# The triangular inverse of a gated delta rule: its levels on the changing half of the columns, eight units per instruction

## The chip, the cores and the metric

The kernel runs on one core of one Trainium2 chip. The time is the device time in microseconds, the median of three runs of the whole program. The profile is one execution of the same program, taken by the hardware profiler.

## The reference

The reference is one attention layer of the gated delta rule with a residual and a layer norm, followed by a feed-forward layer on ternary weights with another residual and layer norm. The input is 8 sequences of 512 tokens with 256 features. There are 16 key heads, each with 2 value heads, of width 128.

The core of it takes the sequence in chunks. For each chunk and head it forms a strictly lower triangular matrix M from the keys, their gates and a decay, and needs T, the inverse of (I - M):

```python
M = -jnp.tril(jnp.einsum('bhnik,bhnjk->bhnij', k_beta, k) * decay, k=-1)
T = solve_triangular(eye - M, jnp.broadcast_to(eye, M.shape), lower=True)
v_new = jnp.einsum('bhnij,bhnjd->bhnid', T, v_beta)
k_cumdecay = jnp.einsum('bhnij,bhnjd->bhnid', T, k_beta * jnp.exp(g)[..., None])
```

A scan over the chunks then carries a state of 128x128 per head: the inverse is applied to the values less what the state predicts, the state is updated with the result, and the output is the part from the state and the part from within the chunk. The kernel uses chunks of C = 128, so 4 chunks per sequence.

## The kernel before

The program has three blocks: the gates, the delta rule, the feed-forward layer. The delta rule is a loop over 128 items, one for each of 16 key heads and 8 sequences. An item has 4 chunks and 2 heads, so 8 units of 128x128.

Each pass of the loop works on three items at once, in three streams. "early" prepares the next item: splitting operands, four projections K, Q, V0, V1 (L516), the projection z (L526), tap and convolution, norms, transposes, Gram matrices (L553). "late" inverts the current item's matrices. "back" runs the recurrence of the item before: per chunk the state product `ks_mm` (L631), the residual (L893), the product with the inverse `y` (L647), its copy `y_copy` (L779), the state update (L660, L910), the query products (L637, L673) and the output; then the norm `o_norm` (L929), transposes `o_turn` (L686) and the output product (L693). `qs_mm` is L637, `intra` is L673.

The inverse is built by doubling. It starts with blocks of 2x2 and has six levels, l = 0 to 5; level l joins blocks of size s = 2 << l into blocks of 2s. U and T, its transpose, are held in f16 in `u16_` and `t16_`, the rounded matrix in `a16`. A level has three products, each on eight units: P from `a16` and T (L593); then, after a mask has picked the off-diagonal blocks of P into `pl[l]`, which is preset to the identity (L865), the new T from U and `pl[l]` (L603) and the new U from `pl[l]` and U (L607). The eight units are handled as two groups g0 and g1 of four, since four units of 128 columns in f32 fill one bank of PSUM, the memory that TensorE writes to. So a level has 6 batches of four matmuls, two predicated copies on VectorE, and four copies back: T of g0 on VectorE (L870), T of g1 (L768) and both U (L771) on ScalarE. After the last level a residual product (L617) and a correction (L624) sharpen the result.

Every engine executes its steps in one fixed order, written out by hand in `ORDER`, with `level(l)` for levels 0 to 3, where the recurrence of the item before lies between the steps. Levels 4 and 5 lie among the projections K, Q and V0 of the next item. Semaphores guard each hand-over: `p_mm`, `p_ready`, `t_mm`, `u_mm`, `t_ready`, `u_ready`.

## Time and profile before

| | us |
|---|---|
| median of 3 runs | 5981.18 |
| lowest, highest | 5980.92, 5990.64 |
| span of the profiled execution | 5983.6 |
| TensorE busy | 5351.0 (89%) |
| VectorE busy | 4743.2 (79%) |
| ScalarE busy | 4155.5 (69%) |
| GpSimd busy | 3081.8 (52%) |

The span is the time from the first to the last instruction of the profiled execution; no other time of that execution is given. An engine's busy time is the union of its instructions' records. A matmul's record holds its own latency, and records overlap when matmuls follow each other, so starts tell more than lengths: "x4" with 0.39 us is four matmuls whose last record ends 0.39 us after the first one's start. "PEld" is the load of the stationary operand. An engine's idle time is listed with what ended it.

### The profile page before, as it was taken

To read this page: it belongs to the slowest core of one execution; us is meant where nothing else is said; L and a number is where in the kernel's file an instruction comes from. 1 tells how busy PE (TensorE), PEld (TensorE's weight loads), DVE (VectorE), ACT (ScalarE), POOL (GpSimd) and SP (SyncE) were. 2 spreads that over 40 slices of the span, in tenths; PEclk is the share of its full clock that TensorE was granted. 3 is DMA by queue.
4 is the path that set the end of the run, shared out by engine and by line. 5 is a ranking of instruction groups with operands and counts; after the bars stand their busy time and mean duration, and the time that the engine had idled before them with its cause. 6 is when DMAs were issued, how large, how long until landed. Compare 5 with 4: busy or idle time off the path is not lost. (4 is left out here: it accounts for less than half of the span.)

```text
span 5983.6 us, 146544 instructions
## 1 busy us (share of the span) xinstructions
PE 5351.0 (89%) x45450; PEld 4415.7 (74%) x45578; DVE 4743.2 (79%) x8288; ACT 4155.5 (69%) x10963; POOL 3081.8 (52%) x3690
## 2 busy tenths in 40 slices
PE   2899999999999999999999999999999999999867
PEld 2677777777777777777777777777777777777756
DVE  4788888888888888888888888888888888888754
ACT  1677777777777777777777777777777777777634
POOL 0555555555555555555555555555555555555434
PEclk8999999999999999999999999999999999999988
DMA  3010101010101010100101010101010101010000
GB/s 105 31 36 27 36 27 36 27 36 27 36 27 36 27 36 27 36 27 30 32 27 36 27 36 27 36 27 36 27 36 27 36 27 36 27 36 27 18 29 21
DMA packets 130814, 194.64 MB, mean 33 GB/s; under 512 B 13344, under 2 KB 61600, under 8 KB 130464
## 3 DMA queue, kind: packets, MB, share of 16 engines
q1 hardware_dynamic: 129312, 190.78, 10.0%
q14 instruction: 325, 2.66, 0.1%
q10 hardware_dynamic: 1152, 0.79, 0.1%
q8 instruction: 25, 0.41, 0.0%
HBM read 185.75 MB, written 5.77 MB: 32 GB/s over the span
## 5 line engine op out<-in xcount | busy, mean ns | idle before, releaser
L865 DVE CAST_PREDICATED pl<-masks,pa 128x512 f16<-128x512 uint16 x1536 | 983.6, 683 | 84.3 <-PE pa L593 84.2
L771 ACT ACTIVATE u<-pa 128x512 f16<-128x512 f32 x1536 | 924.5, 602 | 16.2 <-PE pa L607 8.2
L824 DVE SCALAR_TENSOR_TENSOR conv<-pb,cws,conv 128x511 f32<-128x511 f32 (+2 forms) x1152 | 831.5, 740 | 65.6 <-ACT conv L714 65.6
L1001 POOL TENSOR_TENSOR xo<-xo,zs 128x512 f32<-128x512 f32 x256 | 327.5, 1279 | 745.1 <-DVE xo L923 745.1
L516 PE MATMUL pb<-xb,wb 128*128 128x512 f32 x2304 | 626.6, 407 | 1.7 <-POOL xb L995 1.7
L603 PE MATMUL pa<-pl,u 128*128 128x128 f16 x6144 | 602.7, 221 | 3.0 <-DVE pl L865 3.0
L607 PE MATMUL pa<-u,pl 128*128 128x128 f16 x6144 | 595.1, 219 | 0.0
L779 ACT ACTIVATE yb<-pb 128x256 f32<-128x256 f32 x512 | 196.7, 384 | 531.2 <-PE pb L647 372.5
L593 PE MATMUL pa<-t,a 128*128 128x128 f16 x6144 | 495.4, 220 | 73.7 <-DVE t L858 72.8
L870 DVE CAST t<-pa 128x512 f16<-128x512 f32 x768 | 527.1, 686 | 1.7 <-PE pa L603 1.3
L593 PEld LDWEIGHTS pa<-t,a 128*128 128x128 f16 x6144 | 388.3, 98 | 189.8 <-DVE attn L838 48.3
L603 PEld LDWEIGHTS pa<-pl,u 128*128 128x128 f16 x6144 | 395.0, 98 | 148.7 <-issue 76.2
L768 ACT ACTIVATE t<-pa 128x512 f16<-128x512 f32 x768 | 462.4, 602 | 57.0 <-PE pa L603 53.1
L693 PE MATMUL pb<-wout,xt 128*128 (+1 forms) x2048 | 493.1, 384 | 2.1 <-ACT xt L800 2.1
L714 ACT ACTIVATE conv<-pb,cws 128x512 f32<-128x512 f32 x384 | 265.2, 691 | 322.0 <-PE pb L516 317.5
L516 PEld LDWEIGHTS pb<-xb,wb 128*128 128x128 f32 x2304 | 405.8, 189 | 68.4 <-POOL xb L995 2.0
L607 PEld LDWEIGHTS pa<-u,pl 128*128 128x128 f16 x6144 | 408.8, 98 | 0.0
L693 PEld LDWEIGHTS pb<-wout,xt 128*128 128x128 f32 x2048 | 370.2, 191 | 42.8 <-ACT xt L800 2.8
L526 PE MATMUL pa<-wb,xb 128*128 128x256 f32 x3072 | 399.6, 286 | 0.0
L893 DVE SCALAR_TENSOR_TENSOR res<-pb,small,vt 128x128 f32<-128x128 f32 x768 | 234.1, 346 | 187.8 <-PE pb L631 183.8
L526 PEld LDWEIGHTS pa<-wb,xb 128*128 128x128 f32 x3072 | 376.1, 191 | 0.0
L647 PE MATMUL pb<-res,u 128*128 128x128 f32 x2048 | 336.9, 287 | 31.2 <-DVE res L889 30.5
(171 smaller groups left out, 13882.1 us busy)
## 6 DMA issues: line engine op xcount, KB each, us to landing
tokn<-in_Wqkvz SPq DMA_DIRECT2D x256, 256.0 KB, 2.7
conv<-in_xT SPq DMA_DIRECT2D x256, 256.0 KB, 3.3
conv<-in_Wqkvz SPq DMA_DIRECT2D x128, 256.0 KB, 2.8
gxb<-in_xT SPq DMA_DIRECT2D x8, 512.0 KB, 3.6
wout<-in_W_out SPq DMA_DIRECT2D x1, 4096.0 KB, 17.7
yacc<-in_x_tok SPq DMA_DIRECT2D x2, 2048.0 KB, 20.6
out<-fob SPq DMA_DIRECT2D x8, 512.0 KB, 2.9
lrow<-rows_scratch SPq DMA_DIRECT2D x128, 6.0 KB
```

Source lines behind the costliest of these rows:

```text
L516: last = nc.tensor.matmul(proj_bank[c][:, :], wb[:, pw, k * WCOL + c * D:k * WCOL + (c + 1) * D], xb[:, px, k * S:(k + 1) * S], start=(i = ...
L526: last = nc.tensor.matmul(proj_bank[4 + g][:, n * R * D:(n + 1) * R * D], xb[:, px, at:at + C], wb[:, pw, k * WCOL + 4 * D:(k + 1) * WCOL] ...
L593: last = nc.tensor.matmul(pa[2 * g + 1][:, u * C:(u + 1) * C], a16[:, 4 * g + u, :], t16_[:, 4 * g + u, :], start=True, stop=True)
L603: last = nc.tensor.matmul(pa[2 * g + 1][:, u * C:(u + 1) * C], u16_[:, 4 * g + u, :], pl[l][:, 4 * g + u, :], start=True, stop=True)
L607: last = nc.tensor.matmul(pa[2 * g][:, u * C:(u + 1) * C], pl[l][:, 4 * g + u, :], u16_[:, 4 * g + u, :], start=True, stop=True)
L647: last = nc.tensor.matmul(pb[0][:, h * D:(h + 1) * D], u32[p][:, unit(n, h), :], res[:, h, :], start=True, stop=True)
L693: last = nc.tensor.matmul(pb[3][:, i * H:(i + 1) * H], xt[:, unit(2 * g + i, h), :], wout[:, ds((b // B) * R + h, 1), :].rearrange("p a n ...
L768: nc.scalar.activation(group(t16_, g), four(pa[2 * g + 1]), ACT.Copy)\
L771: nc.scalar.activation(group(u16_, g), four(pa[2 * g]), ACT.Copy).then_inc(u_ready[g].sem, 1)
L824: nc.vector.scalar_tensor_tensor(out=conv[c][:, back:S], in0=proj_bank[c][:, 0:S - back], scalar=cws[p][:, c * TAPS + 3 - back:c * TAPS + ...
L865: nc.vector.copy_predicated(group(pl[l], g), masks[:, l:l + 1, :].broadcast_to([128, 4, C]), four(pa[2 * g + 1])).then_inc(p_ready.sem, 1)
L870: nc.vector.tensor_copy(group(t16_, 0), four(pa[1])).then_inc(t_ready[0].sem, 1)
```

## The change

A level changes only half of the columns: of T those of the first block of each pair, of U those of the second. After the change the products P, T and U of a level stream just these 64 columns of each unit, and write them packed, so that all eight units (8 x 64 = 512 values in f32) fit in one bank: P in `pa[3]`, T in `pa[1]`, U in `pa[0]`. Each product has one copy for all eight units, that spreads the packed columns back to their places: `halves(t, l, odd)` takes of every unit the pieces of s = 2 << l elements that lie 2s apart. The predicated copy stays on VectorE, both copies back are ScalarE's, and the second group's waits are gone or merged. T and U become separate steps, with the state update of the recurrence between them. In the diff, lines of the order table beyond these and lines that only pass names on are left out.

```diff
+        def halves(t, l, odd):
+
+            return t[:, :, :].rearrange("p u (b w s) -> p u b w s", w=2, s=2 << l)[:, :, :, odd, :]
+
+        def half_unit(t, u, l, odd):
+
+            return t[:, u, :].rearrange("p (b w s) -> p b w s", w=2, s=2 << l)[:, :, odd, :]
+
+        def packed(bank, l):
+
+            return bank[:, :].rearrange("p (u b s) -> p u b s", u=NU, s=2 << l)
+
+        def packed_unit(bank, u):
+
+            return bank[:, u * (C // 2):(u + 1) * (C // 2)]
...
-        u_first, t_first_mm, p_mm, p_ready, t_mm, u_mm = signal("u_first", 2), signal("t_first_mm", 2), signal("p_mm", 12), signal("p_ready", 12), signal("t_mm", 12), signal("u_mm", 12)
-        u_ready = [signal(f"u_ready{g}", LEVELS) for g in range(2)]
-        t_ready = [signal(f"t_ready{g}", LEVELS + 1) for g in range(2)]
+        u_first, t_first_mm, p_mm, p_ready, t_mm, u_mm = signal("u_first", 2), signal("t_first_mm", 2), signal("p_mm", LEVELS), signal("p_ready", LEVELS), signal("t_mm", LEVELS), signal("u_mm", LEVELS)
+        u_ready, t_ready, t_first_ready = signal("u_ready", LEVELS), signal("t_ready", LEVELS), signal("t_first_ready", 2)
+        p_bank, t_bank, u_bank = pa[3], pa[1], pa[0]
...
-                    + (back(("q_part", l)) if l and chain else []) + late(("p", l), ("ut_mm", 2 * l)) + (back(("update_mm", l)) if l < NC - 1 else [])
-                    + late(("ut_mm", 2 * l + 1)) + (back(("intra_mm", l)) if chain else []) + sum(between, []) + late(("ut", l))
+                    + (back(("q_part", l)) if l and chain else []) + late(("p", l), ("t_mm", l)) + (back(("update_mm", l)) if l < NC - 1 else [])
+                    + late(("u_mm", l)) + (back(("intra_mm", l)) if chain else []) + sum(between, []) + late(("t_copy", l), ("u_copy", l))
...
             def p_product(a, p, l):
-                for g in range(2):
-                    pe.wait_ge(t_ready[g].sem, t_ready[g].at(a, l + 1))
-                    if l == 0 and g == 0:
-                        pe.wait_ge(attn_ready.sem, attn_ready.at(a, 2))
-                    if l == 0 and g == 1:
-                        pe.wait_ge(vt_ready.sem, vt_ready.at(a, 1))
-                    for u in range(4):
-                        last = nc.tensor.matmul(pa[2 * g + 1][:, u * C:(u + 1) * C], a16[:, 4 * g + u, :],
-                                                t16_[:, 4 * g + u, :], start=True, stop=True)
-                    last.then_inc(p_mm.sem, 1)
-
-            def ut_product(a, p, i):
-                l, g = i // 2, i % 2
-                pe.wait_ge(p_ready.sem, p_ready.at(a, i + 1))
+                if l == 0:
+                    pe.wait_ge(t_first_ready.sem, t_first_ready.at(a, 2))
+                    pe.wait_ge(attn_ready.sem, attn_ready.at(a, 2))
+                    pe.wait_ge(vt_ready.sem, vt_ready.at(a, 1))
+                else:
+                    pe.wait_ge(t_ready.sem, t_ready.at(a, l))
+                for u in range(NU):
+                    last = nc.tensor.matmul(packed_unit(p_bank, u), a16[:, u, :], half_unit(t16_, u, l, 0), start=True, stop=True)
+                last.then_inc(p_mm.sem, 1)
+
+            def t_product(a, p, l):
+                pe.wait_ge(p_ready.sem, p_ready.at(a, l + 1))
                 if l:
-                    pe.wait_ge(u_ready[g].sem, u_ready[g].at(a, l))
-                for u in range(4):
-                    last = nc.tensor.matmul(pa[2 * g + 1][:, u * C:(u + 1) * C], u16_[:, 4 * g + u, :],
-                                            pl[l][:, 4 * g + u, :], start=True, stop=True)
+                    pe.wait_ge(u_ready.sem, u_ready.at(a, l))
+                for u in range(NU):
+                    last = nc.tensor.matmul(packed_unit(t_bank, u), u16_[:, u, :], half_unit(pl[l], u, l, 0), start=True, stop=True)
                 last.then_inc(t_mm.sem, 1)
-                for u in range(4):
-                    last = nc.tensor.matmul(pa[2 * g][:, u * C:(u + 1) * C], pl[l][:, 4 * g + u, :], u16_[:, 4 * g + u, :],
-                                            start=True, stop=True)
+
+            def u_product(a, p, l):
+                for u in range(NU):
+                    last = nc.tensor.matmul(packed_unit(u_bank, u), pl[l][:, u, :], half_unit(u16_, u, l, 1), start=True, stop=True)
                 last.then_inc(u_mm.sem, 1)
 
             def resid_product(a, p, g):
-                pe.wait_ge(t_ready[g].sem, t_ready[g].at(a, LEVELS + 1))
-                pe.wait_ge(u_ready[g].sem, u_ready[g].at(a, LEVELS))
+                pe.wait_ge(t_ready.sem, t_ready.at(a, LEVELS))
+                pe.wait_ge(u_ready.sem, u_ready.at(a, LEVELS))
...
-            def ut(a, p, l):
-                for g in range(2):
-                    if g == 1:
-                        act.wait_ge(t_mm.sem, t_mm.at(a, 2 * l + 2))
-                        nc.scalar.activation(group(t16_, g), four(pa[2 * g + 1]), ACT.Copy)\
-                            .then_inc(t_ready[g].sem, 1)
-                    act.wait_ge(u_mm.sem, u_mm.at(a, 2 * l + g + 1))
-                    nc.scalar.activation(group(u16_, g), four(pa[2 * g]), ACT.Copy).then_inc(u_ready[g].sem, 1)
+                                         ACT.Copy).then_inc(t_first_ready.sem, 1)
+
+            def t_copy(a, p, l):
+                act.wait_ge(t_mm.sem, t_mm.at(a, l + 1))
+                nc.scalar.activation(halves(t16_, l, 0), packed(t_bank, l), ACT.Copy).then_inc(t_ready.sem, 1)
+
+            def u_copy(a, p, l):
+                act.wait_ge(u_mm.sem, u_mm.at(a, l + 1))
+                nc.scalar.activation(halves(u16_, l, 1), packed(u_bank, l), ACT.Copy).then_inc(u_ready.sem, 1)
...
             def factor(a, p, l):
-                for g in range(2):
-                    ve.wait_ge(p_mm.sem, p_mm.at(a, 2 * l + g + 1))
-                    ve.sem_inc(passed[0].sem, 1)
-                    nc.vector.copy_predicated(group(pl[l], g), masks[:, l:l + 1, :].broadcast_to([128, 4, C]),
-                                              four(pa[2 * g + 1])).then_inc(p_ready.sem, 1)
-
-            def ut(a, p, l):
-                ve.wait_ge(t_mm.sem, t_mm.at(a, 2 * l + 1))
-                nc.vector.tensor_copy(group(t16_, 0), four(pa[1])).then_inc(t_ready[0].sem, 1)
...
```

The first place is the end of level 0 on TensorE, where L660 is the state update and L673 the intra product. Before:

```order
L603 MATMUL pa1<-pl0,u16 128x128 x4
L607 MATMUL pa0<-u16,pl0 128x128 x4
L660 MATMUL pb2<-yb,kw0 128x128 x2
L603 MATMUL pa3<-pl0,u16 128x128 x4
L607 MATMUL pa2<-u16,pl0 128x128 x4
L673 MATMUL pb1<-yb,attn0 128x128 x2
L564 MATMUL pb3<-neg,identb 128x512
L569 MATMUL pb3<-rrow,lrow 128x128 x4
```

and now, where L617 is T, L622 U, L674 the update and L687 intra:

```order
L617 MATMUL pa1<-pl0,u16 128x64 x8
L674 MATMUL pb2<-yb,kw0 128x128 x2
L622 MATMUL pa0<-u16,pl0 128x64 x8
L687 MATMUL pb1<-yb,attn0 128x128 x2
L580 MATMUL pb3<-neg,identb 128x512
L585 MATMUL pb3<-rrow,lrow 128x128 x4
```

Behind the update stood T and U of group 1; now U of all eight units stands there, and T stands ahead of the update.

The second place is VectorE in levels 4 and 5, from the predicated copy of level 4 through `o_norm` (L929) to the first convolutions (L824). Before:

```order
L865 COPY_PREDICATED pl4<-masks,pa1 128x512
L865 COPY_PREDICATED pl4<-masks,pa3 128x512
L929 TENSOR_TENSOR xo<-xo,rr 128x512
L870 CAST t16<-pa1 128x512
L865 COPY_PREDICATED pl5<-masks,pa1 128x512
L865 COPY_PREDICATED pl5<-masks,pa3 128x512
L824 SCALAR_TENSOR_TENSOR conv0<-pb0,cws0,conv0 128x511
L824 SCALAR_TENSOR_TENSOR conv1<-pb1,cws0,conv1 128x511
L870 CAST t16<-pa1 128x512
L824 SCALAR_TENSOR_TENSOR conv0<-pb0,cws0,conv0 128x510
```

and now, where L878 is the predicated copy, L938 `o_norm` and L837 the convolutions:

```order
L878 COPY_PREDICATED pl4<-masks,pa3 128x16x32
L938 TENSOR_TENSOR xo<-xo,rr 128x512
L878 COPY_PREDICATED pl5<-masks,pa3 128x8x64
L837 SCALAR_TENSOR_TENSOR conv0<-pb0,cws0,conv0 128x511
L837 SCALAR_TENSOR_TENSOR conv1<-pb1,cws0,conv1 128x511
L837 SCALAR_TENSOR_TENSOR conv0<-pb0,cws0,conv0 128x510
L837 SCALAR_TENSOR_TENSOR conv1<-pb1,cws0,conv1 128x510
```

One predicated copy stands for two, and the T copies (L870), one behind `o_norm` and one between the convolutions, are gone from this engine.

## Rows read from the trace of the kernel before

**Rows 1.** The page, busy time (share of the span) and instructions by engine:

```profile
PE 5351.0 (89%) x45450; PEld 4415.7 (74%) x45578; DVE 4743.2 (79%) x8288; ACT 4155.5 (69%) x10963; POOL 3081.8 (52%) x3690
```

**Rows 2.** One millisecond: its ends, length, busy time by engine, granted clock, DMA:

```profile
1000.00:2000.00 1000.00, 922.92 (x8041) 761.93 (x8064) 822.07 (x1468) 730.78 (x1935) 538.58 (x649) 1.00 0.10 31
```

**Rows 3.** Groups by line, 1000 to 5000 us: busy us, mean ns, idle before:

```profile
L865 DVE CAST_PREDICATED pl<-masks,pa 128x512 f16<-128x512 uint16 x1117 | 715.2, 683 | 56.1 <-PE pa L593 56.1
...
L870 DVE CAST t<-pa 128x512 f16<-128x512 f32 x558 | 383.0, 686 | 0.2
```

**Rows 4.** Timeline, TensorE, level 2: start us, us, instruction, idle before:

```profile
2508.58 0.70 PE L631 MATMUL pb<-st,kq 128*128 128x256 f32 x2
...
2510.05 0.64 PE L647 MATMUL pb<-res,u 128*128 128x128 f32 x4
...
2511.16 0.71 PE L660 MATMUL pb<-yb,kw 128*128 128x128 f32 x4
...
2512.66 0.62 PE L631 MATMUL pb<-st,kq 128*128 128x256 f32 x2
```

**Rows 5.** Timeline, VectorE, level 2:

```profile
2509.31 0.61 DVE L893 SCALAR_TENSOR_TENSOR res<-pb,small,vt 128x128 f32<-128x128 f32 x2 [0.75 <-PE pb L631]
```

**Rows 6.** Timeline, ScalarE, level 2:

```profile
2510.73 0.38 ACT L779 ACTIVATE yb<-pb 128x256 f32<-128x256 f32 x1 [1.45 <-PE pb L647]
```

**Rows 7.** Timeline, TensorE, end of level 0 of the next item:

```profile
2544.75 0.39 PE L603 MATMUL pa<-pl,u 128*128 128x128 f16 x4
...
2546.01 0.39 PE L569 MATMUL pb<-rrow,lrow 6*128 6x128 bf16 x4
2546.33 0.70 PE L631 MATMUL pb<-st,kq 128*128 128x256 f32 x2
```

**Rows 8.** Timeline, TensorE, levels 4 and 5:

```profile
2516.29 0.76 PE L593 MATMUL pa<-t,a 128*128 128x128 f16 x8
2516.87 1.63 PE L516 MATMUL pb<-xb,wb 128*128 128x512 f32 x6
2518.34 0.40 PE L603 MATMUL pa<-pl,u 128*128 128x128 f16 x4
...
2519.54 0.65 PE L686 MATMUL pb<-ident,xo 128*128 128x128 f32 x4
...
2520.54 1.64 PE L516 MATMUL pb<-xb,wb 128*128 128x512 f32 x6
...
2522.90 1.61 PE L516 MATMUL pb<-xb,wb 128*128 128x512 f32 x6
2524.61 0.22 PE L617 MATMUL pa<-t,a 128*128 128x128 f16 x1
```

**Rows 9.** Timeline, VectorE, levels 4 and 5 and the convolutions behind:

```profile
2516.84 1.29 DVE L865 CAST_PREDICATED pl<-masks,pa 128x512 f16<-128x512 uint16 x2
2518.04 1.37 DVE L929 TENSOR_TENSOR xo<-xo,rr 128x512 f32<-128x512 f32 x1
2519.33 0.68 DVE L870 CAST t<-pa 128x512 f16<-128x512 f32 x1
...
2523.02 0.75 DVE L824 SCALAR_TENSOR_TENSOR conv<-pb,cws,conv 128x511 f32<-128x511 f32 x1 [0.46 <-ACT conv L714]
...
2530.50 0.74 DVE L824 SCALAR_TENSOR_TENSOR conv<-pb,cws,conv 128x511 f32<-128x511 f32 x1
```

**Rows 10.** Weight loads by line: duration ns least, median, longest:

```profile
L603 PEld LDWEIGHTS pa<-pl,u x6144: 95/98/152, 180.7 to 5657.6; 128*128 128x128 f16 x199
...
L536 PEld LDWEIGHTS pb<-ident,conv x1536: 137/140/143, 166.0 to 5633.5; 128*128 128x128 f32 x192
```

**Rows 11.** Timeline, GpSimd, the power for the output's norm:

```profile
2516.58 1.02 POOL L1008 TENSOR_TENSOR rr<-rse,expo_eps 128x4 f32<-128x4 f32 x1
```

**Rows 12.** Timeline, ScalarE, level 5: tap Q and the copies:

```profile
2522.30 0.69 ACT L714 ACTIVATE conv<-pb,cws 128x512 f32<-128x512 f32 x1 [1.04 <-PE pb L516]
...
...
2523.84 0.61 ACT L771 ACTIVATE u<-pa 128x512 f16<-128x512 f32 x1
```

More of the change, by code:

```diff
@@ L458, in delta_rule @@
             + level(3) + back(("gate", g1)) + early(("split", 4)) + late(("p_mm", 4))
-            + early(("project", K)) + late(("p", 4), ("ut_mm", 8), ("ut_mm", 9)) + back(("o_norm", g0)) + early(("tap", K)) + late(("ut", 4))
-            + back(("o_turn", g0), ("x_copy", g0)) + late(("p_mm", 5)) + early(("project", Q)) + late(("p", 5), ("ut_mm", 10), ("ut_mm", 11))
-            + early(("tap", Q), ("conv", 0)) + late(("ut", 5)) + back(("o_square", g1), ("o_rnorm", g1)) + early(("conv", 1), ("project", V0))
+            + early(("project", K)) + late(("p", 4), ("t_mm", 4), ("u_mm", 4)) + back(("o_norm", g0)) + early(("tap", K)) + late(("t_copy", 4), ("u_copy", 4))
+            + back(("o_turn", g0), ("x_copy", g0)) + late(("p_mm", 5)) + early(("project", Q)) + late(("p", 5), ("t_mm", 5), ("u_mm", 5))
+            + early(("tap", Q), ("conv", 0)) + late(("t_copy", 5), ("u_copy", 5)) + back(("o_square", g1), ("o_rnorm", g1)) + early(("conv", 1), ("project", V0))
             + late(("resid_mm", g0), ("resid_mm", g1), ("resid", g0), ("resid", g1)) + back(("out_mm", g0)) + early(("conv", 2), ("tap", V0)) + back(("o_norm", g1), ("added", g0))
@@ L801, in _ @@
             steps(act, tap=tap, silu=silu, z=z, squares=norm_squares, vt=values, kq=keys_queries, decay=decay,
-                  rounded=rounded, t_first=t_first, ut=ut, y_copy=y_copy, q_part=q_part, o_square=o_square, x_copy=x_copy)
+                  rounded=rounded, t_first=t_first, t_copy=t_copy, u_copy=u_copy, y_copy=y_copy, q_part=q_part, o_square=o_square, x_copy=x_copy)
         @block.vector
@@ L858, in t_first @@
                     nc.vector.tensor_copy(group(t16_, 0), pa[0][:, :].bitcast(f16)[:, 0:512].rearrange("p (u c) -> p u c", u=4))\
-                        .then_inc(t_ready[0].sem, 1)
+                        .then_inc(t_first_ready.sem, 1)
             def factor(a, p, l):
-                for g in range(2):
-                    ve.wait_ge(p_mm.sem, p_mm.at(a, 2 * l + g + 1))
-                    ve.sem_inc(passed[0].sem, 1)
-                    nc.vector.copy_predicated(group(pl[l], g), masks[:, l:l + 1, :].broadcast_to([128, 4, C]),
-                                              four(pa[2 * g + 1])).then_inc(p_ready.sem, 1)
-            def ut(a, p, l):
-                ve.wait_ge(t_mm.sem, t_mm.at(a, 2 * l + 1))
-                nc.vector.tensor_copy(group(t16_, 0), four(pa[1])).then_inc(t_ready[0].sem, 1)
+                ve.wait_ge(p_mm.sem, p_mm.at(a, l + 1))
+                ve.sem_inc(passed[0].sem, 1)
+                mask = masks[:, l, :].rearrange("p (b w s) -> p b w s", w=2, s=2 << l)[:, :, 0, :]
+                nc.vector.copy_predicated(halves(pl[l], l, 0), mask[:, None, :, :].broadcast_to([128, NU, C // (4 << l), 2 << l]),
+                                          packed(p_bank, l)).then_inc(p_ready.sem, 1)
             def resid(a, p, g):
@@ L938, in _ @@
             steps(ve, conv=convolve, normed=norm, system=system, attn=attention, u_first=first, t_first=t_first, p=factor,
-                  ut=ut, resid=resid, fix=fix, residual=residual, y=y, state=state, out=output, o_norm=o_norm, added=add)
+                  resid=resid, fix=fix, residual=residual, y=y, state=state, out=output, o_norm=o_norm, added=add)
         @block.gpsimd
```

3 lines of the change are left out of this document (1 added, 2 removed).

## The prediction

> **What bounds the kernel now.** I read the page first for shares, then the busy time by stretches for a typical millisecond, then the groups by line, then the timeline of one item, engine by engine; the last decides. The page gives TensorE 89%, VectorE 79%, ScalarE 69% and no idle engine [rows 1]; a steady millisecond has TensorE at 92%, at the granted clock 1.00, which is 2.4 GHz [rows 2]. An average does not say which wait ends last, so first the scale: the T copy of group 0 (L870) runs 6 times an item and 558 times in 4000 us [rows 3], so an item takes 4000 / 93 = 43.0 us, and 128 items make 5504 us of the span of 5983.6 us. Only the item is touched.
>
> A modelled matmul record ends late, so I read starts. In [rows 8] the rows of L603 x4 record 0.39 to 0.40 us: one matmul of 0.22 plus three spacings, so f16 matmuls on 128 columns start 0.056 us apart; eight take 0.45 us, and a level's 24 take 1.34 us.
>
> In levels 0 to 2 the recurrence of the item before runs beside the inverse: state product L631, residual on VectorE, y product L647, copy yb on ScalarE, update L660, state on VectorE. Level 2 takes 4.08 us from one L631 to the next [rows 4]. The residual starts at 2509.31 and lasts 0.61 [rows 5], y starts at 2510.05; yb starts at 2510.73 and lasts 0.38 [rows 6], L660 starts 0.05 later. This loop hides most of the inverse. In levels 0 and 1 TensorE's own queue behind L660 is longer than the loop: group 1's T and U stand there, 0.45 us, ahead of intra, the decay products and the next L631 [rows 7].
>
> From level 3's end to the residual product L617 no recurrence is left, and the inverse's own queue sets the time: 8.32 us from the P of level 4 (2516.29) to L617 (2524.61) [rows 8]. Behind it VectorE runs almost without a gap from 2523.02 to the second convolutions at 2530.50 [rows 9], which the normalization, the Gram product and the next item wait for. So both TensorE and VectorE must gain there.
>
> **The change, part by part.** Per item 144 matmuls keep their weights and lose half their columns. Matmuls on 64 columns in f16 are not in the trace. Upper bound: 0.056 us, spacing unchanged. Lower: half, 0.028. The weight load decides. Recorded loads are 98 ns for f16 and 140 ns for the single-pass transposes of f32 [rows 10]; a pass of 128 columns takes some 0.056, so a record of 140 has about 84 ns beside it, and the f16 load has 98 - 84 = 14 ns, an estimate well under 28. I take 0.030, so 0.24 us for eight.
>
> VectorE loses six of twelve predicated copies (0.60 us each in the queue: a pair records 1.29 where one is 0.68 [rows 3, 9]) and all six T copies; ScalarE goes from 18 to 12 copies of about 0.60 [rows 12]. The new copies have 512 elements as before, written in pieces of 64 down to 2 elements. No row has pieces so short. Lower bound: the same 0.60 to 0.68 us; upper: double, as o_norm L929 takes 1.37 us for 512 elements where the T copy takes 0.68 [rows 9]. I take the same, since PSUM is read without gaps and the count is equal.
>
> The "SBUF — State Buffer" page of the Trainium skill (section "Door 1: The DMA port swizzle", its note on cachelines) says that full bandwidth wants at least two accesses per 16-byte line. The shortest pieces still use four of a line's eight f16 elements, so by that rule the copies keep their duration; a rule that charged each change of line would lead to the rival on pieces. No row of the trace decides it.
>
> - Levels 0 and 1: behind L660 the queue holds U alone, 0.24, in place of T and U of group 1, 0.45: 0.21 each. T is issued before L660, while TensorE waits for yb, so moving it ahead costs nothing. In level 1 the y product also starts 0.07 earlier, since P is shorter and the residual (end 2509.92 in the same place of level 2) becomes its last wait. Sum 0.49.
> - Level 2: 0.07 for y likewise, and L631 follows the state instead of the queue: 2512.66 becomes 0.08 less. Sum 0.15.
> - Level 3 to the K projection: intra waits for the query part, 0.07 earlier and with less ahead of it in the queue: 2515.62. P of level 4 starts at 2516.10, takes 0.24 and no longer pauses for group 1's T copy, and the projection starts at about 2516.40 instead of 2516.87 [rows 8]: 0.47.
> - Level 4: T starts when the projection ends (about 1.3 us later, 2517.72) because the one predicated copy ends at 2517.4. T and U end at 2518.2. The output's transposes L686 then wait for o_norm, which waits for GpSimd's power (2516.58 + 1.02 [rows 11]), so it ends at about 2518.9, and L686 starts at 2518.95. P of level 5 needs a T copy that on VectorE stood behind o_norm, 2519.33 to 2520.01 [rows 9]. Now it is ScalarE's, behind tap K: about 2518.75 to 2519.35. P starts at 2519.42, projection Q at 2519.68 against 2520.54: 0.86.
> - Level 5: T and U (0.48) follow the projection at 2521.0, V0 starts at 2521.5 instead of 2522.90. But L617 waits for ScalarE: tap Q starts 1.76 us after its projection (2520.54 to 2522.30 [rows 12]), so 2521.44; with 0.59 for it, 0.48 for the T copy and 0.61 for the U copy the last ends at 2523.1. Before, it ended at 2523.84 + 0.61 = 2524.45 [rows 12]. L617: 2523.15 against 2524.61, 1.46 us.
> - VectorE behind it: the second convolution of the first pair starts 0.86 earlier, as its tap does, and a T copy of 0.60 is gone from the dense queue: 1.46 at L824 of 2530.50. Both engines arrive equally early, and what follows keeps its length.
>
> Sum per item 0.49 + 0.15 + 1.46 = 2.10 us, times 128 = 269 us. The span would be 5983.6 - 269 = 5715; the median of the runs is 2.4 us below this span, so 5712 us. Waits that the change adds: the first P waits for both transposed groups and the values' copy at once, but TensorE's only work there is this P and a y product that waits for VectorE's residual. What is late next is ScalarE (two copies behind each tap) and GpSimd's power behind the norm.
>
> A rule that speaks against the gain: "TensorE: Matmul & The Clock Gate" (LDWEIGHTS) of the Trainium skill gives a load as columns over 1.2, 107 ns for 128, unless the fast weight load applies, for which it names non-f32 weights. The trace contradicts 107 ns as a spacing, with 0.056 us. In between, a load bound of 0.056 remains possible, and that is the first rival.
>
> **The rivals.**
> First, the weight load bounds and 64 columns cost as much as 128. For it: every spacing measured has one load per matmul, and even loads of six rows record 0.39 us for four in this trace's decay products [rows 7]. Against: the 42 ns above. Then levels 0 to 2 gain nothing, since behind L660 the U of all eight units costs what T and U of group 1 cost. The projections K and Q start at 2516.57 (0.30) and 2519.90 (0.64), V0 at 2522.1 (0.80); ScalarE's last copy ends at 2523.35, V0 1.3 after its start, so L617 is at 2523.6, 1.0 earlier. Sum 1.0, times 128 = 128: 5853 us.
>
> Second, the other side: the short pieces double the copies, on both engines, to 1.2 us. For it: no such form in the trace. Against: the f32 to f16 conversion itself costs ScalarE nothing visible (L771 takes 0.61 us, L714 with f32 output 0.69 [rows 12]). T of levels 0 and 1 then delays L660 by 0.2, eating their gain; in level 2 ScalarE has yb, query part, two copies and the squares, about 4.1 us for a level of 3.9: 0.2 lost. P of level 4 starts 0.36 late; P of level 5 0.38 late; behind it predicated copy, T, then tap Q and two copies of 1.2 put L617 at 2525.5, 0.9 late. Net 1.0 us lost an item: 5981 + 128 = 6109 us. Between 0.6 (gain 2.1) and 1.2 (loss 1.0) the sign changes near 1.0 us a copy: from there on it is slower.
>
> Third, the relief on VectorE and TensorE doesn't travel: the stage behind the convolutions waits for GpSimd or ScalarE instead. Then the 1.46 shrinks to about half, with the levels' 0.64 whole: 1.4 times 128 = 175, 5806 us. Against: GpSimd is 52% busy [rows 1], and its power waits on ScalarE's squares, which also come earlier.
>
> **How the numbers follow.** Forecast 5712 us: 0.55. Weight load bound, 5853: 0.20. Relief half lost, 5806: 0.12. Slower by the pieces, 6109: 0.06. The remaining 0.07 is a larger gain, down to about 5640, if the levels' unseen gaps ("issue") shrink with the number of waits. The walk has some 0.3 us an item of doubt, 40 us, so the forecast's own range is 5670 to 5755. The range from 5645 to 5870 holds the forecast and both rivals on its side, and leaves out the slower case and the tails. A difference below 0.2% (12 us) can't be told from none. Faster 0.92: all cases but the pieces, less a little for copies near 1.0 us; same 0.02; slower 0.06.
>
> **What would show it right or wrong.** Right: eight P matmuls record about 0.40 us (0.22 less half of 0.056, and seven spacings of 0.030) and not 0.58; predicated copies and both ScalarE copies at 0.60 to 0.69 us in every form; L660 of levels 0 and 1 followed by the next state product 0.2 us sooner; the residual product, which followed the start of level 4's P by 8.32 us, now some 7.05 us behind it; TensorE's clock still 1.00. Wrong: copies of the 2-element form over 1 us; idle time of VectorE growing by all of the 7.2 us an item (12 times 0.60) that leave it while the item stays at 43 us; a granted clock under 1.00 in the levels.

## The result and the profile after

The changed kernel takes 5834.04 us (median of 4 runs, 5823.81 to 5838.18) against 5983.61 us for the kernel before, here the median of 4 runs; the ratio is 0.9742, 95% interval 0.9731 to 0.9754. That is 2.6% or some 150 us faster. The forecast was 5712, with 5645 to 5870 as its range: the sign and the range hold, the gain is 55% of the 271 us that were forecast.

The page of the changed kernel, span and busy time by engine, as in [rows 1]:

```profile
span 5836.3 us, 140166 instructions
## 1 busy us (share of the span) xinstructions
PE 5052.9 (87%) x45578; PEld 4068.5 (70%) x45578; DVE 3884.5 (67%) x6752; ACT 3789.3 (65%) x10195; POOL 3079.6 (53%) x3690
```

VectorE lost 859 us of busy time, which is 6.7 us an item, ScalarE 366 us. A TensorE with less work is still the fullest engine. Now the single instructions, first the P matmuls of the levels (durations in ns, least, median, longest), then the predicated copies in all six forms, then the T copies in all six:

```profile
L609 PEld LDWEIGHTS pa<-t,a x6144: 95/98/151, 179.0 to 5504.0; 128*128 128x128 f16 x199
L609 PE MATMUL pa<-t,a x6144: 190/193/261, 179.0 to 5504.1; 128*128 128x64 f16 x199
```

```profile
L878 DVE CAST_PREDICATED pl<-masks,pa x768: 676/691/750, 179.7 to 5504.5; 128x512 f16<-128x512 uint16 x192
```

```profile
L780 ACT ACTIVATE t<-pa x768: 587/597/608, 181.2 to 5505.9; 128x512 f16<-128x512 f32 x192
```

All 768 predicated copies lie between 676 and 750 ns and all T copies between 587 and 608. By level, the predicated copies have medians of 743 ns (pieces of two elements), 722 (pieces of four) and 677 to 691 (longer pieces); the T copies have 597, 607 and 588 without such an order. The slower rival is dead: on ScalarE short pieces cost nothing, on VectorE the two shortest forms cost 0.03 to 0.06 us, far from a doubling. The "SBUF — State Buffer" page of the Trainium skill (section "Door 1: The DMA port swizzle", its note on cachelines) asks for two accesses per line, and such pieces still make four. By that rule nothing is lost; the trace agrees on ScalarE, and on VectorE but for these 0.03 to 0.06 us.

TensorE's timeline from the P of level 4 (L609) to the residual product (L631), which stands against [rows 8]; L532 is a projection, L617 T, L700 the transposes of the output:

```profile
2535.97 0.40 PE L609 MATMUL pa<-t,a 128*128 128x64 f16 x8
2536.20 1.64 PE L532 MATMUL pb<-xb,wb 128*128 128x512 f32 x6
2537.68 0.41 PE L617 MATMUL pa<-pl,u 128*128 128x64 f16 x8
...
2539.20 0.65 PE L700 MATMUL pb<-ident,xo 128*128 128x128 f32 x4 [0.89 <-DVE xo L938]
2539.69 0.40 PE L609 MATMUL pa<-t,a 128*128 128x64 f16 x8
2539.93 1.61 PE L532 MATMUL pb<-xb,wb 128*128 128x512 f32 x6
...
2541.86 1.63 PE L532 MATMUL pb<-xb,wb 128*128 128x512 f32 x6
2543.41 0.22 PE L631 MATMUL pa<-t,a 128*128 128x128 f16 x1
```

Eight matmuls record 0.40 to 0.41 us: 0.193 for one and seven spacings of 0.030. Half the columns cost about half the time (0.030 against 0.056), as estimated, although each weight load still records 98 ns. The first rival is dead too. P of level 4 to residual product: 7.44 us, before 8.32, forecast 7.05. The 0.39 that are missing lie ahead of L700: 0.89 us idle, released by o_norm. VectorE and GpSimd in the same stretch, against [rows 9, 11]:

```profile
2536.52 0.69 DVE L878 CAST_PREDICATED pl<-masks,pa 128x512 f16<-128x512 uint16 x1
2537.30 1.77 DVE L938 TENSOR_TENSOR xo<-xo,rr 128x512 f32<-128x512 f32 x1
2540.24 0.69 DVE L878 CAST_PREDICATED pl<-masks,pa 128x512 f16<-128x512 uint16 x1 [1.17 <-PE pa L609]
...
2542.38 2.06 DVE L837 SCALAR_TENSOR_TENSOR conv<-pb,cws,conv 128x511 f32<-128x511 f32 x3 [0.78 <-ACT conv L728]
```

```profile
2536.25 1.02 POOL L1017 TENSOR_TENSOR rr<-rse,expo_eps 128x4 f32<-128x4 f32 x1
2537.24 1.28 POOL L1010 TENSOR_TENSOR xo<-xo,zs 128x512 f32<-128x512 f32 x1
2538.46 1.08 POOL L1002 CAST wb<-conv 128x512 fp32r<-128x512 f32 x1
```

o_norm (L938) takes 1.77 us, before it took 1.37. GpSimd's gate product (L1010) has the same place as before, right behind the power; in the kernel before it is this row:

```profile
2517.57 1.29 POOL L1001 TENSOR_TENSOR xo<-xo,zs 128x512 f32<-128x512 f32 x1
```

Before, o_norm began 0.47 us behind the start of this product and ended at 2519.41, 0.55 us after its end. Now it begins 0.06 behind it and ends at 2539.07, again 0.55 us after its end. That 0.55 is the median of all 128 such pairs in either trace. So o_norm hardly advanced while the product ran, an earlier start on VectorE only made it longer, and from the P of level 4 to the end of o_norm it takes 3.1 us in both kernels. The GpSimd cast behind the product (L1002) did not hold it: the last 0.55 us ran beside that cast.

Next, a typical millisecond (against [rows 2]), then two items that follow each other, then the first levels of the second; the columns are length, busy time by engine, granted clock, DMA:

```profile
1000.00:2000.00 1000.00, 892.53 (x8277) 718.01 (x8276) 683.67 (x1219) 682.17 (x1834) 555.59 (x671) 0.98 0.10 32
2475.20:2516.30 41.10, 36.77 (x346) 29.58 (x346) 28.70 (x52) 28.65 (x78) 23.23 (x29) 1.00 0.10 33
2516.30:2560.00 43.70, 39.20 (x342) 31.73 (x342) 28.18 (x52) 28.43 (x77) 22.66 (x29) 0.92 0.08 26
2519.00:2525.70 6.70, 6.69 (x39) 5.20 (x40) 2.11 (x5) 2.92 (x4) 1.52 (x2) 0.52 0.00 0
```

The granted clock is 0.98 where it was 1.00. The item from 2475.2 has 1.00 and takes 41.1 us; the next has 0.92 and takes 43.7, and its stretch of 6.70 us in levels 0 and 1 ran at 0.52, so nearly all of it at 1.2 GHz. No term of the forecast had this, though the prediction named a granted clock under 1.00 in the levels as a sign of being wrong. TensorE's timeline there:

```profile
2517.01 0.41 PE L609 MATMUL pa<-t,a 128*128 128x64 f16 x8 [0.77 <-ACT t L775]
2517.76 0.68 PE L661 MATMUL pb<-res,u 128*128 128x128 f32 x4 [0.34 <-DVE res L898]
...
2519.01 0.98 PE L674 MATMUL pb<-yb,kw 128*128 128x128 f32 x4 [0.22 <-ACT yb L792]
2519.78 0.64 PE L622 MATMUL pa<-u,pl 128*128 128x64 f16 x8
2520.22 1.20 PE L687 MATMUL pb<-yb,attn 128*128 128x128 f32 x4
2521.22 0.63 PE L580 MATMUL pb<-neg,identb 128*128 128x512 bf16 x1
...
2522.32 1.22 PE L645 MATMUL pb<-st,kq 128*128 128x256 f32 x2
2523.33 0.63 PE L609 MATMUL pa<-t,a 128*128 128x64 f16 x8
```

P of level 0 waits 0.77 us, y 0.34, the update 0.22, and from 2519.01 on the groups record longer, up to about twice their length (L645 1.22 us where it has 0.70 at full clock, L687 1.20 where it has 0.69). Level 0 takes 6.32 us (2517.01 to 2523.33), against 4.30 in an item at full clock.

I cut both traces into items, from one copy of the first T on VectorE to the next, 117 items each from the middle. The loop's body holds two items, so odd and even items differ:

| kernel | items at clock 1.00: even, odd, us | items at a lower clock | mean of 117, us |
|---|---|---|---|
| before | 42.2, 43.5 to 44.4 | 1 | 43.00 |
| changed | 41.1, 41.5 | 29, of 43.0 or about 44 us | 41.80 |

In the changed trace all 29 low stretches begin about 3 us after the start of an item, in level 0; 15 last 6.8 us and 14 last 3.4 us. 27 of the 29 are in odd items, and the other 31 odd items have the same idle times and keep their clock. In the kernel before nearly all odd items keep it too, although TensorE idles there even longer ahead of the update (median 1.17 us); one of them:

```profile
2498.49 0.62 PE L593 MATMUL pa<-t,a 128*128 128x128 f16 x8 [0.61 <-DVE t L858]
2499.40 0.68 PE L647 MATMUL pb<-res,u 128*128 128x128 f32 x4 [0.29 <-DVE res L889]
2501.73 0.71 PE L660 MATMUL pb<-yb,kw 128*128 128x128 f32 x4 [1.20 <-ACT yb L779]
```

So the length of the gaps alone does not tell when the clock falls.

Two more things stand out. Even items at full clock gained 1.1 us, not 2.1. Odd items gained more, 2.2 at full clock, where the change is the same. And the page's row for fetched instructions changed, before and after:

```profile
q14 instruction: 325, 2.66, 0.1%
```

```profile
q14 instruction: 18, 0.15, 0.0%
```

### The profile page after: what moved, and what is told of

Its sections match the earlier page's. It is cut to its first block and busy times, and to the rows that moved or that the text cites. A ratio compares the mean times of both kernels' runs of the same rounds, so it can differ in the third digit from the quotient of the medians.

```text
span 5836.3 us, 140166 instructions
## 1 busy us (share of the span) xinstructions
PE 5052.9 (87%) x45578; PEld 4068.5 (70%) x45578; DVE 3884.5 (67%) x6752; ACT 3789.3 (65%) x10195; POOL 3079.6 (53%) x3690
## 5 line engine op out<-in xcount | busy, mean ns | idle before, releaser
L837 DVE SCALAR_TENSOR_TENSOR conv<-pb,cws,conv 128x511 f32<-128x511 f32 (+2 forms) x1152 | 819.4, 739 | 112.2 <-ACT conv L728 112.2
L1010 POOL TENSOR_TENSOR xo<-xo,zs 128x512 f32<-128x512 f32 x256 | 326.6, 1276 | 704.0 <-DVE xo L932 704.0
L878 DVE CAST_PREDICATED pl<-masks,pa 128x512 f16<-128x512 uint16 x768 | 538.1, 701 | 168.0 <-PE pa L609 164.3
L532 PE MATMUL pb<-xb,wb 128*128 128x512 f32 x2304 | 627.4, 408 | 1.3 <-POOL xb L1004 1.3
L784 ACT ACTIVATE u<-pa 128x512 f16<-128x512 f32 x768 | 461.3, 601 | 85.2 <-PE pa L622 76.0
L532 PEld LDWEIGHTS pb<-xb,wb 128*128 128x128 f32 x2304 | 407.1, 190 | 68.5 <-POOL xb L1004 1.6
L687 PE MATMUL pb<-yb,attn 128*128 128x128 f32 x2048 | 368.2, 304 | 71.4 <-ACT qe L799 71.4
L661 PEld LDWEIGHTS pb<-res,u 128*128 128x128 f32 x2048 | 276.7, 195 | 185.1 <-DVE res L902 131.1
L609 PEld LDWEIGHTS pa<-t,a 128*128 128x128 f16 x6144 | 279.9, 99 | 178.6 <-issue 63.1
L661 PE MATMUL pb<-res,u 128*128 128x128 f32 x2048 | 368.5, 304 | 37.8 <-DVE res L898 37.1
L919 DVE SCALAR_TENSOR_TENSOR st<-st,small,pb 128x128 f32<-128x128 f32 x512 | 155.1, 345 | 368.0 <-PE pb L674 368.0
L609 PE MATMUL pa<-t,a 128*128 128x64 f16 x6144 | 312.0, 194 | 94.4 <-ACT t L775 93.0
L932 DVE TENSOR_TENSOR xo<-qe,pb 128x256 f32<-128x256 f32 x384 | 161.6, 421 | 292.3 <-PE pb L687 292.2
L969 POOL TENSOR_TENSOR ssqe<-ssq,expo_eps 128x4 f32<-128x4 f32 x256 | 51.0, 199 | 553.9 <-ACT tokn L749 553.9
```

The lines of the kernel that those rows point to most:

```text
L532: last = nc.tensor.matmul(proj_bank[c][:, :], wb[:, pw, k * WCOL + c * D:k * WCOL + (c + 1) * D], xb[:, px, k * S:(k + 1) * S], start=(i = ...
L609: last = nc.tensor.matmul(packed_unit(p_bank, u), a16[:, u, :], half_unit(t16_, u, l, 0), start=True, stop=True)
L661: last = nc.tensor.matmul(pb[0][:, h * D:(h + 1) * D], u32[p][:, unit(n, h), :], res[:, h, :], start=True, stop=True)
L687: last = nc.tensor.matmul(pb[1][:, h * D:(h + 1) * D], attn[p][:, unit(n, h), :], yb[:, h, :], start=True, stop=True)
L784: nc.scalar.activation(halves(u16_, l, 1), packed(u_bank, l), ACT.Copy).then_inc(u_ready.sem, 1)
L837: nc.vector.scalar_tensor_tensor(out=conv[c][:, back:S], in0=proj_bank[c][:, 0:S - back], scalar=cws[p][:, c * TAPS + 3 - back:c * TAPS + ...
```

## The experiments

All ratios are to runs of the kernel before on the same chip. That kernel took 5984 us (e1 to e4), 5988 (e5 to e8) and 5995 (e9 to e11) there, so ratios compare better than times. In what follows "theory A" and the rivals are those of each recorded expectation. Odd and even items are those of the table.

**e1: extra work round the start of level 0.**

```diff
+                    pe.wait_ge(vt_ready.sem, vt_ready.at(a, 1))
+                    for _ in range(3):
+                        filler(pa[3])      # ahead of the wait of level 0's P
                     pe.wait_ge(t_first_ready.sem, t_first_ready.at(a, 2))
                     pe.wait_ge(attn_ready.sem, attn_ready.at(a, 2))
-                    pe.wait_ge(vt_ready.sem, vt_ready.at(a, 1))
...
+                if l == 0:
+                    filler(pa[2])          # behind P, and again behind T
```

> The changed kernel with five extra matmuls per item on TensorE, constants into banks that are free, each a repeat of the 512-column constant product of the decay step (about 0.21 us at the full clock): three before the P of level 0, one behind it, one behind the T of level 0, all where TensorE waits. Theory A (the granted clock): 29 of 117 items of the changed kernel are 1.6 to 2.7 us longer and show a clock of 0.92 or 0.96, and the drop follows the idle stretches round the start of level 0. The extra work fills them, so nearly all items show 1.00 and last 41.0 to 41.5 us; 0.59 us an item comes back, 75 us: about 5759 us. Rival B: the low clock is a symptom of a stretch that other waits make long, or comes from the lighter levels as a whole; then the low items stay, and the extra work costs nothing or up to 1 us an item: 5834 to 5960 us. Rival C: the level chain has no real slack there and the extra matmuls delay it, 5 times 0.21 an item: 5970 us at most.

Measured: 5764.12 us, ratio 0.9629 (0.9613 to 0.9645). All items show 1.00 and alternate between 41.1 and 41.5 us. One millisecond:

```profile
1000.00:2000.00 1000.00, 908.15 (x8466) 723.70 (x8514) 692.12 (x1235) 692.20 (x1859) 560.77 (x677) 1.00 0.10 32
```

Theory A, to 5 us. The lower clock cost the changed kernel 70 us, and the extra work, 1.07 us an item by its expected length, is hidden completely: items at full clock keep their 41.1 and 41.5 us.

**e11: the same work elsewhere, the control.**

```diff
                 last.then_inc(t_mm.sem, 1)
+                if l == 4:
+                    for _ in range(5):
+                        filler(pa[2])
```

> The changed kernel with the same five extra constant matmuls, put behind the T of level 4, ahead of its U, where TensorE is busy on both sides and waits for o_norm only later. It is the control of e1. Theory A (what counts is the idle stretch round the start of level 0): the items with a low clock stay, about 29 of 117, and the extra 1.07 us lie partly in the 0.88 us wait for o_norm, so 0.2 us or more of an item is lost: 5840 to 5880 us. Rival B (any more work on TensorE in an item holds the clock): all items at 1.00, 5834 - 75 + 25 = about 5785 us.

Measured: 5901.91 us, ratio 0.9845 (0.9811 to 0.9878): slower than expected. 51 of 117 items have a lower clock, more than the 29 without the work; the rest still take 41.1 and 41.5. 41 of the 51 are even items, which hardly fell without the work. So more work as such doesn't hold the clock, its place does. Why more items fell than without the work is open.

```profile
1000.00:2000.00 1000.00, 907.04 (x8281) 727.81 (x8328) 679.74 (x1211) 678.17 (x1826) 553.89 (x669) 0.98 0.10 32
```

**e2: o_norm early.**

```diff
-            + early(("decay", g1)) + level(2) + early(("small", 0)) + back(("o_square", g0), ("o_rnorm", g0))
-            + level(3) + back(("gate", g1)) ...
+            + early(("decay", g1)) + level(2) + back(("o_square", g0), ("o_rnorm", g0)) + early(("small", 0))
+            + level(3, back(("o_norm", g0))) + back(("gate", g1)) ...
```

> The changed kernel with the output norm of the first half moved in the order table: its GpSimd power ahead of the copies of the small factors, and its multiplication o_norm on VectorE from behind the predicated copy of level 4 to behind that of level 3, where VectorE is idle for 2 us. Theory A: the transposes of the output on TensorE wait 0.88 us for o_norm, which takes 1.77 us because it falls wholly beside GpSimd's gate product; early it takes about 0.68 and the wait goes: 0.9 us an item off the way from the P of level 4 to the residual product (7.36 us now), 115 us: 5720 us, if the clock stays as it is. Rival B: something else ends at the same time (the U copy on ScalarE behind tap K, ending 0.1 us before P of level 5), and only 0.3 us an item comes: 5795 us. Rival C: TensorE is idle elsewhere then and the clock drops in more items, so less than half of the gain remains.

Measured: 5722.34 us, ratio 0.956 (0.9545 to 0.9576), 112 us under the changed kernel. All o_norm now take the short time:

```profile
L938 DVE TENSOR_TENSOR xo<-xo,rr x256: 675/691/694, 233.7 to 5428.4; 128x512 f32<-128x512 f32 x128
```

Items at full clock take 40.5 and 41.0, so 0.55 us of it are the wait; 20 items instead of 29 have a lower clock, and none a clock of 0.92, which gives the rest. P of level 4 to residual product is 6.80 us (2528.63 to 2535.43). The size of the total is theory A's, but some 40 of the 112 us came by the clock.

**e3: both.**

> Both edits together: the five extra constant matmuls round the start of level 0 and the early o_norm. If both theories hold the gains add: 5834 - 75 - 115 = 5644 us. If the clock is the cause of most of the difference to the forecast and o_norm of the rest, this kernel is near or below the 5712 us of the forecast. If either rival holds, it lies at 5700 to 5760 us.

Measured: 5694.06 us, ratio 0.9514 (0.9498 to 0.953), the fastest of all. Items take 40.5 and 41.0, all at 1.00. The gains of e1 and e2, 70 and 112 us, don't add to 182 but to 140, since part of e2's was clock. The expectation was missed by 50 us. The time is under the forecast's 5712, but by way of the instruction fetch that e9 shows, which the forecast did not have.

```profile
1000.00:2000.00 1000.00, 919.82 (x8568) 731.18 (x8615) 679.00 (x1253) 699.77 (x1903) 558.31 (x689) 1.00 0.10 32
```

**e5: the columns of before, issued as pairs.**

```diff
                 for u in range(NU):
+                    for _ in range(2):
                         last = nc.tensor.matmul(packed_unit(p_bank, u), a16[:, u, :], ...   # T and U likewise
```

> The changed kernel with each P, T and U matmul of the levels issued twice in a row with the same operands and target, so TensorE streams as many columns per level as before the change (24 spacings of 0.056 us, or 48 of 0.030). Copies and waits are unchanged. Theory A: the halved columns are worth what the forecast gave them as the difference to its first rival, 1.0 us an item (0.2 behind the update in levels 0 and 1, the rest before the projections), and the denser TensorE keeps its clock, which gives back 0.59: 5834 + 128 - 75 = 5887 us. Rival B: TensorE's columns are hidden behind the recurrence and VectorE, and the whole gain came from the copies; then only the clock is seen: 5760 us. Rival C: the clock does not come back, since the idle stretch before level 0 is unchanged: 5960 us.

Measured: 6245.58 us, ratio 1.0431 (1.0403 to 1.0458). No expectation held: TensorE's loop body grew by 288 matmuls, and now it is TensorE's that is fetched. The fetches, and the idle time of TensorE at the P of level 0 that nothing releases (us in total, times, longest):

```profile
q8 instruction: 641, 10.50, 0.7%
```

```profile
PEld pa L610 <- issue: 257.6, 63, 5.1
PE pa L610 <- issue: 246.2, 61, 4.9
```

So odd items cost up to 5 us more and are no measure. Most even items (51 of 59) are untouched by it and show a clock of 1.00: 42.6 us against 41.1. So TensorE's spacings are worth up to 1.5 us an item. That is an upper figure, since 48 spacings of 0.030 make 1.44 us a level where the kernel before had 1.34, and it can't be told from the 1.1 us an item by which the forecast lies under its first rival.

**e6: the T copy on VectorE.**

```diff
-                act.wait_ge(t_mm.sem, t_mm.at(a, l + 1))
-                nc.scalar.activation(halves(t16_, l, 0), packed(t_bank, l), ACT.Copy).then_inc(t_ready.sem, 1)
+                ve.wait_ge(t_mm.sem, t_mm.at(a, l + 1))
+                nc.vector.tensor_copy(halves(t16_, l, 0), packed(t_bank, l)).then_inc(t_ready.sem, 1)
```

> The changed kernel with the T copy of each level on VectorE instead of ScalarE, at the same place of the order table; all eight units in one copy of 512 elements as now. Theory A: behind level 5 VectorE's queue is dense, and a copy between the first and second convolutions delays all behind it by 0.60 us, as the forecast said for the copy that the change removed; levels 0 to 4 hide theirs (in level 4 it stands behind o_norm and ends when ScalarE's does): 77 us more, 5911 us. Rival B: VectorE has slack behind level 5 now (it waits 0.78 us for tap Q), ScalarE is relieved, and nothing is lost: 5834 us within 20. Rival C: in levels 1 and 2 the copy delays the state update as well, 0.2 to 0.4 us each: over 5950 us.

Measured: 5999.59 us, ratio 1.0017 (1.0007 to 1.0027): 165 us lost, the whole gain. Items at full clock take 41.6 and 42.0, about 0.5 more, near theory A's 0.60. In even items the P of level 4 comes when it did, so levels 0 to 3 hide their copies; 0.43 us are lost from there to the residual product and 0.14 behind it. But 76 of 117 items now have a lower clock, and that more than doubles the price.

**e4, e7, e8: the loop bodies.** The change shortened ScalarE's and VectorE's loop bodies. The three kernels pad them back with semaphore increments.

```diff
+                    for _ in range(13):                                 # e4: ScalarE, behind the value SiLU, in the loop and ahead of it
+                        act.sem_inc(passed[2].sem, 1)
...
+                if l == 0:                                              # e7: ScalarE, behind the T copy
+                    for _ in range(6 if isinstance(a, int) else 13):
+                        act.sem_inc(passed[2].sem, 1)
...
+                if l == 0:                                              # e8: VectorE, behind the predicated copy
+                    for _ in range(18 if isinstance(a, int) else 20):
+                        ve.sem_inc(passed[2].sem, 1)
```

> The changed kernel with 13 semaphore increments per item on ScalarE, behind the second value SiLU, where ScalarE waits 1.44 us for GpSimd. They do no work and stand for the instructions that the change took from ScalarE's loop body. In the trace of before every second item is 1.5 us longer (43.7 against 42.2 us), with an idle time of 2.8 us of ScalarE that nothing releases, at the first instruction behind the loop's branch, and 325 packets of instructions are fetched; after the change it is 41.5 against 41.1 and 18 packets. Theory A: the loop body of ScalarE now fits where instructions are held and is no longer fetched anew at each turn; padded back to its old length the packets come back to about 325 and every second item is 1.1 to 1.5 us longer: 70 to 96 us more, 5905 to 5930 us. Rival B: the difference between odd and even items came from the order of ScalarE's copies; then padding costs at most the increments themselves, hidden in the idle time: 5834 us within 12, and packets stay near 18.

> The changed kernel with semaphore increments on ScalarE behind the T copy of level 0, where it waits 1.0 us for TensorE: 6 per item ahead of the loop and 13 in it, so that ScalarE's loop body has the same length (248 instructions) and begins at the same place of its program as before the change. The padding of the earlier run had the length and began 27 instructions later, and fetched nothing. Theory A: whether a loop body is fetched anew depends on where it lies as well as on its length, and ScalarE's was: some 300 packets of instructions come back, ScalarE idles 2.8 us behind the branch, every second item is 1.1 us longer than now: 5834 + 70 = 5904 us. Rival B: the fetch was VectorE's: packets stay near 18 and the time at 5834 us within 20.

> The changed kernel with semaphore increments on VectorE behind the predicated copy of level 0, where it waits 1.7 us for TensorE: 18 per item ahead of the loop and 20 in it, so that VectorE's loop body has the same length (246 instructions) and begins at the same place of its program as before the change. Theory A (the fetch was ScalarE's): packets stay near 18, time 5834 us within 20. Rival B (the fetch was VectorE's): some 300 packets come back and every second item is longer: about 5904 us. If neither this nor the run padded on ScalarE fetches, the extra length of every second item has another cause.

Measured: e4 5843.94 us (0.9754, 0.9733 to 0.9774), e8 5830.19 us (0.9735, 0.9718 to 0.9751), both as the changed kernel, with 19 packets each: theory A of e4 failed, the old length alone doesn't bring the fetch back. e7: 5998.0 us (1.0018, 1.0009 to 1.0028). The row of e7's fetches and that of ScalarE's wait at the first copy yb behind the branch, and the same wait in the kernel before:

```profile
q14 instruction: 324, 2.65, 0.1%
```

```profile
ACT yb L795 <- issue: 164.0, 58, 3.1
```

```profile
ACT yb L779 <- issue: 153.4, 55, 3.3
```

The fetch was ScalarE's, and not the length alone but the place decides: 248 instructions in both e4 and e7, 27 apart. In e7 the padding also stands elsewhere in the body; e9 moves the body and nothing else. It costs more than I expected. Even items stay at 41.1, but every odd one has a lower clock and takes 45.5 us on average. Put where the old one lay, the loop body takes away the change's whole gain.

"Runtime: NRT & Kernel Launch" of the Trainium skill (section "Instruction fetch mechanics") says that a taken branch whose target is not among the two blocks held forces a fetch before execution goes on. The stall of 2.8 us behind the branch agrees.

**e9: the kernel before, moved by 27 instructions.**

```diff
             act.wait_ge(made.sem, made.at(0, MADE))
+            for _ in range(27):
+                act.sem_inc(passed[2].sem, 1)
```

> The kernel before the change, with nothing added but 27 semaphore increments on ScalarE once, ahead of all items. ScalarE's loop body keeps its 248 instructions and begins 27 instructions later, where the padded loop of e4 began, which fetched nothing. Theory A (the place of ScalarE's loop body decides whether it is fetched at each turn, and the kernel before paid for it): packets of instructions fall from 325 to about 18, every second item falls from 43.7 to about 42.6 us, the others stay at 42.2: 0.55 us an item, 70 us less: about 5914 us. Then half of what the change brought was this. Rival B: the place matters in the changed kernel only, or the fetch is hidden here: 5984 us within 12.

Measured: 5920.18 us, ratio 0.9876 (0.986 to 0.9893). Items take 42.2 and 42.7 us, mean 42.47, all at 1.00, and the fetches are gone:

```profile
q14 instruction: 21, 0.16, 0.0%
```

The pair shows the place alone: 27 idle instructions, executed once, are worth 1.2%.

**e10: fetch and extra work together.**

> The changed kernel with both the ScalarE padding of e7 (which brought 324 packets back and cost 164 us) and the five extra constant matmuls of e1. Theory A: the fetch by itself costs every second item about 1.1 to 1.5 us at the full clock, as it did before the change, and the rest of the 164 us is clock: the stall of ScalarE leaves TensorE idle round the start of level 0 and all 58 items behind a turn run part of the levels at 1.2 GHz. With the extra matmuls most of them are back at 1.00: items of 41.1 and 42.6 to 43.0 us, 5834 to 5880 us. Rival B: the extra matmuls lie ahead of the stall, which still idles TensorE for 1.2 us, so the clock still falls in most of these items: over 5930 us. Rival C: the 164 us are the fetch alone: no change from 5998 us.

Measured: 5842.24 us, ratio 0.9749 (0.9733 to 0.9766). Items take 41.1 and 42.4 to 43.0, one of 117 has a lower clock:

```profile
1000.00:2000.00 1000.00, 894.67 (x8316) 712.76 (x8363) 680.58 (x1213) 678.71 (x1822) 554.56 (x669) 1.00 0.10 32
```

Theory A. The fetch alone costs an odd item 0.9 to 1.5 us, 1.1 in the median; the rest of e7's 164 us was the clock, and the extra matmuls bring it back although they stand ahead of the stall.

## Why the prediction was right, and where its sizes were wrong

The direction, the places and the prices of single instructions were right: spacing 0.030, copies at 0.60 to 0.70 us (0.74 for the shortest pieces on VectorE), both rivals on prices dead. At full clock and without the fetch (e9 to e1, so 0.9876 to 0.9629) the change is worth 2.5%, 148 us or 1.2 us an item. The forecast's sum was 2.10. How the 1.2 us divide between fewer columns and fewer copies is not shown: e5 and e6 each take one of them back, but not cleanly.

- Levels 0 to 2, forecast 0.64: from the first y to the state product of level 3 an even item took 12.11 us, now 11.66: 0.45. Levels 0 and 1 gained 0.18 and 0.19 against 0.21 and 0.28, level 2 0.08 against 0.15.
- Level 3 to the residual product, forecast 1.46: 11.81 us, now 11.07: 0.74. This term failed, at two steps. The larger is o_norm: the forecast let it keep its 1.37 us and end earlier, but its end hangs on GpSimd's gate product, 0.55 us behind it in both kernels, so it stayed 3.1 us behind the P of level 4 where the forecast had 2.8. From that P to the residual product 0.82 us came, not 1.27. The other is level 3: the P of level 4 should have come 0.19 earlier and came 0.09 later, since intra still waits for ScalarE's query part. With o_norm out of the way (e3 against e1: 0.9629 to 0.9514) 69 us come. Even so change and move make 217 us together (e9 to e3), short of the 269; 5712 is passed only with the 74 us of the fetch.
- The same o_norm stood as evidence for the second rival, 1.37 us where a copy takes 0.68. Beside no gate product it takes 0.69 (e2), so its length said nothing of access patterns.
- P of level 0 now waits for both transposed groups, and starts about 0.16 us later. As forecast, this wait is free for the item at full clock: the first y starts 1.26 us after the first T copy in both kernels. But in odd items it lengthens the idle time ahead of this P from 0.61 to 0.77 us.
- Behind the residual product to the next item's start an even item takes 17.0 us in both kernels. So what was gained ahead travels in full, and the third rival, which put a loss there, is wrong in its place, though its loss of half of the 1.46 and its engine, GpSimd, fit.
- Not in the sum: the clock, 70 us lost (e1). The prediction read 1.00 in [rows 2] and asked for it again among the signs of being right, but had no price for a drop. And the instruction fetch, 74 us gained (e9), which could have been read: the page has 325 packets of instructions, and ScalarE's first copy behind the branch waits 2.8 us for nothing that the profile shows, in 55 of 63 turns.

So the 150 us are 148 for the change, 74 for a place in the program and 70 back for the clock. That these add up is no proof, since each is the step from one kernel to the next along before, e9, e1, changed. The change's 148 us alone would put the time at 5836, inside the range, so the range holds by the mechanism. It is luck that the two unseen terms cancel: with the clock's loss alone the time would be near 5906, outside. In number the first rival, 5853, was nearest to 5834, and its mechanism is the one that the spacing of 0.030 refutes.

## What to carry to other kernels

Where a change makes the fullest engine lighter, look where it then idles in a row, and put a price on a drop of its clock; work without use in such a gap can be worth more than it costs. When an instruction is to start earlier, ask what sets its end: one that runs beside another engine's work may only get longer, and then the other engine's chain has to move. And before a gain is put down to a change, count the fetched instructions: a loop that grows, shrinks or only moves can gain or lose a per cent by itself.

## What the runs showed of the hardware that was not expected

- TensorE's clock fell to 1.2 GHz in 29 of 117 items, 15 times for 6.8 us and 14 times for 3.4, although no idle stretch in the 15 us ahead was longer than 0.8 us. Five short matmuls in those gaps kept it at 2.4 GHz (e1); the same five some 17 us later did not (e11). Idle time alone doesn't decide: 31 odd items with the same gaps kept their clock, and so did 57 of 58 odd items of the kernel before, with gaps of about 1.2 us. What does decide is open.
- A loop body of 248 instructions on ScalarE is fetched anew at each turn or not at all, depending on where it begins (27 instructions apart), with a stall of about 2.8 us; on TensorE a body that grew by 288 matmuls is fetched where the shorter one was not, with stalls up to 5.1 us.
- A VectorE product of two f32 tensors of 512 elements takes 0.69 us alone. Beside GpSimd's product of such tensors it ends 0.55 us after that one's end, whenever it began: 1.37 us long in the kernel before, 1.77 in the changed one.
- ScalarE copies that spread 512 elements in pieces of two f16 take 597 ns, no more than those in long pieces (588 to 607). VectorE's predicated copies take 743 ns there against 677 to 691.
